# Gate, count and place by groups of batches, norms slot by slot, and a new order of the stages

## The reference

```python
h = _L0_tok_ref(x, L0_tok_W, L0_tok_b)                       # 36 image patches per batch
h = jnp.concatenate([h, _L0_txt_ref(x_txt, L0_txt_W)], axis=1)
h = h + _L0_attn_ref(_layernorm(h, axis=-1), ...)            # q, k, v, relu(scores), FFN 64-128-64, layernorm
h = h + _L0_ffn_ref(_layernorm(h, axis=-1), ...)             # top-1 of 8 experts, with a capacity
h = h + _L1_attn_ref(_layernorm(h, axis=-1), ...)            # 16 heads, linear attention, gelu
h = h + _L1_ffn_ref(_layernorm(h, axis=-1), ...)             # top-2 of 8 experts, 64-256-64, gelu
```

```python
idx = jnp.argmax(probs, axis=-1)
one_hot = jax.nn.one_hot(idx, E, dtype=jnp.float32)
pos = (jnp.cumsum(one_hot, axis=0) * one_hot).sum(-1).astype(jnp.int32) - 1
kept = pos < C
buf = jnp.zeros((E, C, D), dtype=h.dtype).at[idx, pos_safe].set(x, mode='drop')
```

## Time and profile before

| | us |
|---|---|
| three runs | 926.06, 931.81, 937.85 |
| median | 931.81 |
| profiled execution | 930.97 |
| its span in the trace | 929.1 |
| outside the span | 1.9 |

### The profile page before, as it was taken

How to read it: one execution, slowest core, us unless ns; L and a number is a source line. 1 busy time by engine, 2 the same in 40 slices (tenths; PEclk the granted TensorE clock), 3 DMA queues, 4 the chain that set the end, 5 groups by cost and what they waited for, 6 DMA issues and landing times.

```text
span 929.1 us, 16212 instructions
## 1 busy us (share of the span) xinstructions
PE 772.0 (83%) x4934; PEld 561.4 (60%) x4934; DVE 613.0 (66%) x2290; ACT 529.0 (57%) x949; POOL 438.8 (47%) x457
## 2 busy tenths in 40 slices
PE   4599898989988539952558999999999999999996
PEld 2366565655656326631437777767776777777774
DVE  2568977768766715545776676788677777766521
ACT  1366545445452226621237777987778977777752
POOL 3643555663424550017554665766666754422222
PEclk9599989898897559985558999999999999999998
DMA  9300000000000011210001222202222112222220
GB/s 299 134 13 11 10 18 16 17 17 3 3 2 3 3 48 63 95 51 21 6 20 37 51 57 57 58 16 44 57 58 57 47 19 50 57 57 57 56 56 14
DMA packets 43776, 40.79 MB, mean 44 GB/s; under 512 B 19322, under 2 KB 38282, under 8 KB 43306
## 3 DMA queue, kind: packets, MB, share of 16 engines
q1 hardware_dynamic: 34682, 33.41, 14.2%
q0 software_dynamic: 7200, 4.17, 2.2%
q10 hardware_dynamic: 1808, 2.17, 0.7%
HBM read 31.61 MB, written 10.58 MB: 45 GB/s over the span
## 4 chain that ended last, share of the span: by engine, by line
PE 41%; issue 12%; DVE 9%; ACT 6%; POOL 5%; another core or an unknown queue 0%; DVEq 0%; POOLq 0%; ACTq 0%
PE psum L496 8%; PE psum L969 7%; PE psum L970 5%; PE psum L1147 2%; PE psum L471 2%; ACT scratch L581 2%; PE psum L947 2%; POOL uu L357 2%; PE psum L940 2%; POOL prob L397 1%; DVE prob L669 1%; PE psum L934 1%; PE psum L964 1%; PE psum L422 1%; PE psum L1129 1%
## 5 line engine op out<-in xcount | busy, mean ns | idle before, releaser
L581 ACT ACTIVATE scratch<-psum,fb 128x584 f32<-128x584 f32 x256 | 178.6, 745 | 93.3 <-PE psum L970 91.1
L397 POOL TENSOR_TENSOR prob<-prob,scratch 128x292 f32<-128x292 f32 x112 | 84.2, 752 | 136.5 <-DVE scratch L828 132.6
L496 PE MATMUL psum<-scratch,w_fw 128*64 128x256 f32 (+1 forms) x1024 | 144.7, 412 | 0.0
L357 POOL DMA_INDIRECT uu<-expert_out,slot_i x80 | 83.0, 1038 | 85.2 <-DVE H L628 65.6
L969 PE MATMUL psum<-kh,fw_hi 128*128 128x292 f32 x352 | 106.7, 326 | 15.4 <-ACT scratch L581 14.8
L899 POOL DMA_INDIRECT slots_buf<-xt,slot_i x80 | 80.2, 1003 | 82.5 <-DVE slot_i L1539 42.7
L496 PEld LDWEIGHTS psum<-scratch,w_fw 128*64 128x64 f32 x1024 | 97.0, 141 | 20.5 <-issue 0.6
L885 POOL DMA_INDIRECT emb<-in_table,w_ids x64 | 61.9, 966 | 89.7 <-DVE stats L1313 70.1
L828 DVE SCALAR_TENSOR_TENSOR scratch<-psum,w_fb,X 128x292 f32<-128x292 f32 x112 | 57.6, 515 | 62.6 <-PE psum L496 62.1
L970 PE MATMUL psum<-kh,fw_lo 128*128 128x292 f32 x352 | 92.9, 290 | 0.0
L969 PEld LDWEIGHTS psum<-kh,fw_hi 128*128 128x128 f32 x352 | 67.1, 191 | 32.8 <-ACT scratch L581 18.8
(11 more groups left out here) (268 smaller groups left out, 1812.3 us busy)
## 6 DMA issues: line engine op xcount, KB each, us to landing
X<-share_buf SPq DMA_DIRECT2D x16, 584.0 KB, 5.8
X<-share_buf SPq DMA_DIRECT2D x16, 512.0 KB, 7.7
slots_buf<-zeros SPq DMA_DIRECT2D x8, 352.0 KB
X<-slots_buf SPq DMA_DIRECT2D x8, 352.0 KB, 3.2
expert_out<-X SPq DMA_DIRECT2D x8, 352.0 KB, 2.5
out<-H SPq DMA_DIRECT2D x16, 128.0 KB
X<-in_patches ACTq DMA_DIRECT2D x1, 1728.0 KB
slots_buf<-xt,slot_i POOLq DMA_INDIRECT x80
```

The source lines that it names most:

```text
L357: pool.indirect_dma_start(yg[b % 2][0:rows, s, :], None, expert_out, bass.IndirectOffsetOnAxis(slot_i[0:rows, b, s:s + 1], 0), bounds_chec ...
L397: pool.tensor_tensor(total[b % 2], total[b % 2], part[m % PARTS], ALU.add).then_inc(sem("summed"), 1)
L496: last = pe.matmul(bank(6 + n % 2)[h * D:(h + 1) * D, 0:z], w["fw2"][:, e * J + j, :], hid[(J * n + j) % (J * UNITS)][:, h, 0:z], start=(j ...
L581: act.activation(hid[(J * n + j) % (J * UNITS)], both(2 + 2 * j), ACT.Gelu, bias=fb1[:, e * J + j:e * J + j + 1]).then_inc(sem("gelu"), 1)
```

## The change

Four things are changed, and with them the order.

1. The steps `gate` and `place` of DVE and `count` of PE run once for each group of batches, with `GROUPS` as nine groups: three of three batches, one of two, and five of one. The product `gate` stays one per batch and leaves its 40 columns in bank 7, from column 320 on, beside those of its group. A group's DVE steps work on up to 120 columns. `XT3` goes from four to eight buffers, since a batch's normed tokens now wait for the place of their group before they are scattered.
2. `norm1b`, `norm2b` and `norm3b` work slot by slot: one instruction per slot of 64 columns with the mean and the inverse root as scalars per row, where one instruction on 320 columns took one of the two.
3. The third transpose of each turn is a full 128x128 square like the other two; the tiles get a sixth slot of zeros, set at the start.
4. All tables of the order have new numbers.

```diff
-XT3 = 4
+XT3 = 8
+TURNED = SLOTS + 1
+GROUPS = ((0, 1, 2), (3, 4, 5), (6, 7, 8), (9, 10), (11,), (12,), (13,), (14,), (15,))
+GMAX = 3
+GATE_AT, COUNT_AT = 320, 320
...
-PER = dict(norm1a=11, norm1b=4, qk_low=3, vals=1, resid=1, norm2a=11, norm2b=5, norm3a=10, norm3b=3, gate=6, place=7,
+PER = dict(norm1a=11, norm1b=11, qk_low=3, vals=1, resid=1, norm2a=11, norm2b=11, norm3a=10, norm3b=6, gate=6, place=7,
...
+def group_of(b):
+
+    for g, members in enumerate(GROUPS):
+        if b in members:
+            return g, b == members[-1]
...
-        DVE_ONE = ((27.75, "norm1a"), (54.5, "norm1b"), (98.75, "q_low"), (112.5, "k_low"), (119.5, "vals"), (165.5, "resid"), (205.75, "norm2a"),
...
-        MOE, SQUEEZE_TWO, DOWN_LAG, GELU_LAG, WEIGH_LAG, SUM_LAG = 159.75, {}, 1.25, 0.5, 2.5, 1.5
...
+        DVE_ONE = ((34.25, "norm1a"), (54, "norm1b"), (98.25, "q_low"), (107.25, "k_low"), (128, "vals"), (166, "resid"), (208.5, "norm2a"),
...
+        MOE, SQUEEZE_TWO, DOWN_LAG, GELU_LAG, WEIGH_LAG, SUM_LAG = 162.75, {}, 1.25, 0.5, 2.5, 0.25
...
-                pe.transpose(bank(1)[0:N_IMG, 2 * P:2 * P + D], total[b % 2][0:D, LEFT:RIGHT], ident[0:D, 0:D])
-                pe.transpose(bank(1)[:, 0:P], total[b % 2][:, 0:P], ident[:])
-                pe.transpose(bank(1)[:, P:2 * P], total[b % 2][:, P:2 * P], ident[:]).then_inc(sem("back"), 1)
+                turn_back(pe, total[b % 2], 1).then_inc(sem("back"), 1)
...
+            for i in range(3):
+                last = pe.transpose(bank(k)[:, i * P:(i + 1) * P], src[:, i * P:(i + 1) * P], ident[:])
+            return last
...
-                banks.take(pe, LOW, sem("gate"), b * PER["gate"] + 1)
+
+                g, last_one = group_of(b)
+                k = GATE_AT + (b - GROUPS[g][0]) * SLOTS * E
+                if last_one:
+                    banks.take(pe, LOW, sem("gate"), g * PER["gate"] + 1)
+                else:
+                    banks.take(pe, LOW, sem("xs3"), b + 1)
                 pe.wait_ge(sem("xs3"), b + 1)
-                slots_by(pe, bank(7), xs3[b % 2], w["gw"]).then_inc(sem("gate_prod"), 1)
+                slots_by(pe, bank(7)[:, k + E:k + SLOTS * E], xs3[b % 2], w["gw"], 2)
+                slots_by(pe, bank(7)[:, k:k + E], xs3[b % 2], w["gw"], 3, 2).then_inc(sem("gate_prod"), 1)
 
             def count(b):
 
 
-                banks.take(pe, LOW, sem("place"), b * PER["place"] + 2)
-                pe.wait_ge(sem("gate"), (b + 1) * PER["gate"])
-                o, dst = oh_b[b % 2], bank(7)[:, 0:(SLOTS + 1) * E].rearrange("p (s e) -> p s e", e=E)
-                last = pe.matmul(dst, tri_b[:], o[:], start=True, stop=False, skip_group_check=True)
-                for s in (IMG, 0, 1, 2, 3):
-                    rows = N_IMG if s == IMG else P
-                    first = 0 if s == IMG else s + 1
-                    if first < TXT:
-                        pe.matmul(dst[:, first:TXT, :], ones_b[0:rows, :], bs(o[0:rows, s, :], TXT - first), start=False, stop=False, skip_group_check=True)
-                    last = pe.matmul(dst[:, SLOTS, :], ones_b[0:rows, :], o[0:rows, s, :], start=False, stop=(s == 3), skip_group_check=True)
+                g, last_one = group_of(b)
+                if not last_one:
+                    return
+                n = len(GROUPS[g]) * SLOTS
+                banks.take(pe, LOW, sem("place"), g * PER["place"] + 2)
+                pe.wait_ge(sem("gate"), (g + 1) * PER["gate"])
+                o, dst = oh_b[g % 2], bank(7)[:, COUNT_AT:COUNT_AT + (n + 1) * E].rearrange("p (s e) -> p s e", e=E)
+                pe.matmul(dst[:, 0:n, :], tri_b[:], o[:, 0:n, :], start=True, stop=False, skip_group_check=True)
+                for s in range(n):
+                    counted = ones_img if s % SLOTS == 0 else ones_b
+                    last = pe.matmul(dst[:, s + 1:n + 1, :], counted[:], bs(o[:, s, :], n - s), start=False, stop=(s == n - 1), skip_group_check=True)
...
-                st(dve.tensor_tensor(zt[:], H[:, b], bc(mv1[b % 2][:, :, 0], D), ALU.subtract))
-                st.sync()
-                st(dve.tensor_tensor(xt[b % 2][:], zt[:], bc(rs[:, 1, :], D), ALU.mult))
-                st(dve.tensor_tensor(X[:, b], zt[:], bc(rs[:, 0, :], D), ALU.mult))
+                st.sync()
+                for s in range(SLOTS):
+                    st(dve.tensor_scalar(xt[b % 2][:, s, :], H[:, b, s, :], mv1[b % 2][:, s, 0:1], rs[:, 1, s:s + 1], ALU.subtract, ALU.mult))
+                for s in range(SLOTS):
+                    st(dve.tensor_scalar(X[:, b, s, :], H[:, b, s, :], mv1[b % 2][:, s, 0:1], rs[:, 0, s:s + 1], ALU.subtract, ALU.mult))
...
-                st(dve.tensor_tensor(zt[:], uu[b % 2][:], bc(mv2[b % 2][:, :, 0], D), ALU.subtract))
-                st.sync()
-                st(dve.tensor_tensor(zt[:], zt[:], bc(rs[:, 0, :], D), ALU.mult))
-                st.sync()
-                st(dve.tensor_tensor(zt[:], zt[:], bs(w["fg"][:], SLOTS), ALU.mult))
+                st.sync()
+                for s in range(SLOTS):
+                    st(dve.scalar_tensor_tensor(out=zt[:, s, :], in0=uu[b % 2][:, s, :], scalar=mv2[b % 2][:, s, 0:1], in1=w["fg"][:], op0=ALU.subtract, op1=ALU.mult))
                 st.sync()
                 dve.wait_ge(sem("offset"), b + 1)
-                st(dve.tensor_tensor(H[:, b], H[:, b], zt[:], ALU.add))
+                for s in range(SLOTS):
+                    st(dve.scalar_tensor_tensor(out=H[:, b, s, :], in0=zt[:, s, :], scalar=rs[:, 0, s:s + 1], in1=H[:, b, s, :], op0=ALU.mult, op1=ALU.add))
...
-                st(dve.tensor_tensor(zt[:], H[:, b], bc(mv3[b % 2][:, :, 0], D), ALU.subtract))
-                st.sync()
-                st(dve.tensor_tensor(xt3[b % XT3][:], zt[:], bc(rs[:, 0, :], D), ALU.mult))
+                st.sync()
+                for s in range(SLOTS):
+                    st(dve.tensor_scalar(xt3[b % XT3][:, s, :], H[:, b, s, :], mv3[b % 2][:, s, 0:1], rs[:, 0, s:s + 1], ALU.subtract, ALU.mult))
...
-                st = Steps(dve, sem("gate"), "gate", b)
-                if b >= 2:
-                    dve.wait_ge(sem("place"), (b - 1) * PER["place"])
+                g, last_one = group_of(b)
+                if not last_one:
+                    return
+                n = len(GROUPS[g]) * SLOTS
+                st = Steps(dve, sem("gate"), "gate", g)
                 dve.wait_ge(sem("gate_prod"), b + 1)
-                if b >= 2:
-                    dve.wait_ge(sem("count"), b - 1)
-                st(dve.tensor_tensor(lg[:], bank(7)[:, 0:SLOTS * E].rearrange("p (s e) -> p s e", s=SLOTS), bs(w["gb"][:], SLOTS), ALU.add))
-                st.sync()
...
+                lgs, mxs, eqs = g_lg[:, 0:n, :], g_mx[:, 0:n], g_eq[:, 0:n, :]
+                gaps = gap[:, GROUPS[g][0]:b + 1].rearrange("p b s e -> p (b s) e")
+                st(dve.tensor_tensor(lgs, bank(7)[:, GATE_AT:GATE_AT + n * E].rearrange("p (s e) -> p s e", e=E), bs(w["gb"][:], n), ALU.add))
...
+                st = Steps(dve, sem("place"), "place", g)
+                dve.wait_ge(sem("count"), g + 1)
+                c = bank(7)[:, COUNT_AT:COUNT_AT + (n + 1) * E].rearrange("p (s e) -> p s e", e=E)
+                p, o = pl[:, 0:n, :], ov[:, 0:n, :]
+                to = slot_f[:, GROUPS[g][0]:b + 1, :].rearrange("p b s -> p (b s)")
+                st(dve.tensor_tensor(p, c[:, 0:n, :], bs(carry[:], n), ALU.add))
```

183 lines of the change are left out of this document (94 added, 89 removed).

## The result

The changed kernel took 948.5 us (median of four) beside 928.9 us of the kernel before: a ratio of 1.022, with a 95% interval of 1.019 to 1.026. Forecast were 902 us, with 883 to 929 us as range. Two further measurements of the same kernel, each beside the kernel before on the same chip, gave 0.998 (0.995 to 1.001; 900.7 us beside 903.4) and 1.010 (1.006 to 1.014; 949.4 beside 937.7). So there are two conditions, told apart by the kernel before alone: one in which it takes some 904 us, here called A, and one in which it takes 929 to 938 us, called B. The traces that the forecast read are from B. The record names the chip for all measurements but the first: A was met on three chips (one of them twice), B on one other. Whether the chip itself makes the condition can't be told from that.

A forecast was written before the change was run, and what follows sets the result against it. Gaps and low clock of PE in steady phase one, and PE's gaps in steady phase two, were taken as the time to win: -14 (phase one) - 14 (phase two) - 1 = -29 from 930.97 us, so 902 us, range 883 to 929.

The forecast's parts named there:

- the price of a slot-wise instruction: DVE norms: 0.146 us per 64-column instruction, bounds 0.12 and 0.21, giving DVE 0.7 us per batch back.
- DVE is busy 78%, so the end hardly moves by this alone: Slot-by-slot norms in phase one: effect on the end 0, bounds -2 and +7 us.
- the ceiling of phase one: Steady phase one: 18.0 down to 14.9 us per batch, 25 us over eight batches; half taken, -12.
- only better numbers in the tables can open it: Phase one: PE and DVE, two in-order queues, wait for each other in a loop; new order worth -12 us.
- Rows 4: Profile rows for phase one: PE's count waits for vals up to 1.5 us; DVE idles six times at vals.
- Groups: Gate, place and count per group: 1.6 us per batch less DVE, no time by itself; -2 us for the counts.
- Phase two: New tables, two table loads per batch fewer: -1.2 us per batch, -14 in all, some 27 us between t4s.
- by 0 up to 2.5 us: Phase two: possible growth of gram's 0.54 us wait because roots_kv comes later; +0.2 us was taken.
- Squares: Full third transposes on PE: 0 taken, at the upper end +4 us in phase one and +2 in phase two.
- The hand-off: From phase one's end to the experts, POOL's scatters: change 0, bounds -2 and +4 us.
- D: Rival in phase one: count waits for the group's DVE gate, clock dips, 947 us; chance 0.06 (above 940 us).
- E: Rival: short DVE instructions and POOL hold each other up, phase one gains nothing, 918 to 925 us; 0.17 with B.

The follow-up runs named there:

- wide norms: Changed kernel with norm1b, norm2b and norm3b back on 320 columns per instruction: 879.4 us, 0.974 in A; 925.7 us, 0.983 in B.

## Why the prediction was wrong

*The step that failed first is the price of a slot-wise instruction.* "One of 64 columns 0.73 / 5 = 0.146 us" came from the statistics, which have one input and no scalars per row. The measured price is 0.24 us for tensor_scalar and 0.21 us for scalar_tensor_tensor (1.07 for five). norm1b thus went from 1.6 to 2.6 us with its reciprocal, and all three norms cost DVE 1.4 us per batch by these prices, instead of giving 0.7 back. Measured are 2.0 us per batch. Where the other 0.6 us come from is not split up; some of the slot-wise instructions are stretched beside POOL's work, as the row above shows at its worst. The upper bound (0.21 us, +0.9 us per batch) was too low as well, and it was multiplied by eight batches of sixteen. It was known as a guess: no row had this operation in this size.

*The second is "DVE is busy 78%, so the end hardly moves by this alone".* In A DVE is busy 93 to 94% of the steady part, and work added to it came out as time nearly one to one. The 78% was right for the trace and was thinned by idle time that comes from condition B: in the run with the new tables for phase two alone, which has the phase one of the kernel before and was taken in A, DVE is busy 97.2 of the 104 us from 103 to 207 us. Added work on DVE still cost 24 us in B (changed kernel against wide norms), so even there the share did not tell how much cover DVE had. These 24 us, against a forecast of 0, are the largest single part of the miss; in the first measurement phase one came out 24 us longer instead of 14 shorter.

*The third is the ceiling of phase one.* The 18.0 us per batch against 14.9 us a little later were read as a loop of two queues that a better order opens: "only better numbers in the tables can open it". In A the very same phase one takes 14.8 us per batch (in the run with the new tables for phase two alone, place goes from 133 to 207 us in five batches), at a granted clock of 0.98 instead of 0.89, and ends 33 us earlier. That is as much as the 33.4 us of gaps and low clock that the forecast had added up, without any change of order; and the old and new tables of phase one differ by some 4 us. Why the two batches at 14.9 us escaped is not known, as they lie in the same trace of B. Rows 4 had 16.3 us of DVE idle in front of vals with nothing named as the end, and I named vals' place in the table as its cause. In A, with vals at that same place, this idle time isn't there at all. Such a gap was a thing to leave open.

*Groups* were right in mechanism. 1.6 us of DVE per batch in eleven batches is 17.6 us; 15.7 us (A, wide norms) were measured. But the prediction booked them as no time, because it held DVE not to be the bound, and took 2 us for the counts. It also miscounted them: nine groups make 89 products (3 x 16 + 11 + 5 x 6) instead of 160, not 105, which at its own 0.05 us is 3.6 us. In B the gain of the groups was not measured.

*Phase two* was forecast at -14 and its tables came to -7 us (5 to 9 us) on the kernel before. Its period from t4 to t4 fell from 28.2 to 27.7 us, not to 27. The wait of `up` for ACT went, as forecast, but gram's wait grew from 0.54 to 1.6 us per batch in the first trace of the changed kernel (row below, from 530 to 810 us), not by 0.2. The bound was there ("by 0 up to 2.5 us"), the value taken was not. What then makes phase two shorter by some 0.5 us per batch and more is not the table loads (moving `roots_kv` back changed nothing), and it stays open.

```profile
PE psum L436 <- DVE scratch L689: 17.6, 11, 2.0
```

*Squares:* nothing that shows in A, as forecast. *The hand-off* from the last place to the first expert product is 12.5 us in A (306.84 to 319.35 us), beside 13.7 us in the first trace of the kernel before. It is 13.7 us in A too (293.06 to 306.71 us, in the run with the new tables for phase two alone), so the 1.2 us go with the kernel and not with the condition.

Of the rivals, D (count waits for the group's gate) happens, but the changed kernel with wide norms has the same groups and is at 0.974, so it doesn't decide. That its 947 us stands beside the measured 948.5 is luck: in B too the same groups with wide norms come to 925.7 us. Waits from 103 to 350 us in the first trace of the changed kernel:

```profile
POOL slots_buf L912 <- DVE slot_i L1572: 84.0, 7, 32.5
...
PE psum L1125 <- DVE oh_b L1547: 12.8, 7, 4.4
```

The first row is POOL's wait for the place of a group in front of its scatters, up to 32.5 us; it alone holds no other engine up as far as these rows show. E had the right place, DVE's short instructions, and for the most part the wrong reason: their plain length, not meetings with POOL. No rival had the combination that was measured. Three of the forecast's own signs of being wrong came: DVE's pieces of 64 columns over 0.2 us, PE's waits for the group's gate in front of count (12.8 us), and gram waiting over 1.5 us per batch. That 902 us was nearly met in A (900.7 us) is chance. The medians of A make a chain there: 903.5 us for the kernel before, -5.3 for the squares, the buffers and the new count, -3.1 for the tables of both phases, -15.7 for the groups, +21.3 for the norms. None of these steps has the size that the forecast gave it, and the base is another than the one that it stood on.

In B wide norms gain 24 us as well. The changed kernel is at 1.010 and 1.022 of the kernel before in B and at 0.998 in A; the difference, 1.2 to 2.4%, fits the 10 to 14 us that B costs phase one more with groups than without. That the late signals of phase one need the scatters, and that B's loss in phase one goes with them, is shown for the changed kernel (50 us). That grouped scatters, up to 15 in a train, cost more than five at a time is likely from the traces, but argued, not shown.

## What to carry to other kernels

Price an instruction by the row of the same operation with the same kind of operands; where none is there, bound it by the dearest neighbour of that size, and ask how the end would stand if the engine were the bound after all. Replacing wide instructions with a broadcast operand by narrow ones with scalars per row lost in both norms that were tried alone: in norm1b three instructions of 0.49 us on 320 columns are cheaper than ten of 0.24, and in norm2b even four are than ten of 0.21. An engine's busy share in one trace doesn't tell how much more it can take: 78% in B was 93% in A. And idle time whose end the profile can't name is no evidence for an order that is wrong: look at whether the same program shows it in another run first.

## What was unexpected of the hardware

- The same program on the same inputs took 904 us or 938 us, depending on the measurement; for the changed kernel it was 900.7 or 949.4 us, with 47 of the 49 us in phase one. In the slow condition ACT and DVE see PE's signals up to 7 us after the products are recorded, mostly while POOL issues indirect scatters, and leaving those out removes it (353.6 to 303.9 us for the last place). Why, and whether it is the chip or something around it, is open.
- Five tensor_scalar on 128x64 floats in SBUF with two scalars per row take 1.21 us, five statistics on the same size 0.73 us, one tensor_tensor of 128x320 0.49 us.
- Five short DVE instructions with two SBUF inputs took 5.92 us instead of 1.07 beside a POOL instruction on 2048 columns that took 4.54 us.
